# Four edits joined in a twelve-layer kernel: two exponentials on GpSimd, a summary in 64-column tiles, a second projection bank, and an earlier normalisation

## The reference, cut to what matters

```
L1_xattn: k = ctx @ Wk.T + bk; v = ctx @ Wv.T + bv           # ctx: 2 x 2048 tokens
          p = exp(clip(q.k / 4, -50, 50)) * keep; out = (p @ v) / (sum p + 1e-8)
L2_attn : attn = softmax(q k^T * scale); out = attn @ v; out @ wo      # 16 heads
L2_ffn  : h = down(silu(up(x))); q = W_q h; top-8 of 45 + 45 keys per head -> 8 experts for each of 8 heads
          z = h . down_embed[idx];  z = silu(z * softmax(sc));  x += z @ up_embed[idx]
L3_xattn: k' = relu(Wkf k) * mask; kv = k'^T v; k_sum = sum k'
          out = (q' kv) / (q' k_sum + 1e-8)                   # q' = relu(Wqf q), 2 x 2048 context tokens
```

## Time and profile before

| what | value |
|---|---|
| median of 3 runs | 1339.32 us (1335.14 to 1339.72) |
| profiled execution, its own time | 1336.76 us |
| its span, first to last instruction | 1334.9 us |
| busy share PE / DVE / ACT / POOL | 85% / 52% / 36% / 12% |
| mean granted TensorE clock | 0.919 of full speed |
| L1X, front to the last tile | 142 to 290 us |
| L2A, loop of units | 783 to 846 us |
| L2F with L3X | 847 to 1161 us |

### The profile page before, as it was taken

One profiled execution on the slowest core, in us unless ns is written; L12 is line 12 of the kernel. 1 busy time (PEld: TensorE's weight loads), 2 busy tenths in 40 slices (PEclk: granted clock), 3 DMA queues, 4 the chain that ended last, 5 costly groups with the idle time before them and its releaser, 6 DMA issues.

```text
span 1334.9 us, 22850 instructions
## 1 busy us (share of the span) xinstructions
PE 1140.2 (85%) x9353; PEld 817.2 (61%) x9353; DVE 696.4 (52%) x1532; ACT 482.1 (36%) x1069; POOL 165.4 (12%) x168
## 2 busy tenths in 40 slices
PE   6987889977877999999999977856986976777998
PEld 5866556656654555555556655735764755676886
DVE  3543456763326777655666253462626647374332
ACT  1101146762312355655566833222332321121322
POOL 0004000000001000000000000073635462000000
PEclk9998999998987999999999999977978957786999
DMA  9021200003003000000000020152524241003552
GB/s 365 1 95 48 111 1 1 2 2 154 0 16 135 1 2 2 1 2 1 2 2 2 2 77 1 54 145 63 152 70 123 78 113 48 14 0 158 198 204 81
DMA packets 16182, 84.38 MB, mean 63 GB/s; under 512 B 3152, under 2 KB 3664, under 8 KB 12368
## 3 DMA queue, kind: packets, MB, share of 16 engines
q1 hardware_dynamic: 7888, 57.75, 11.3%
q0 software_dynamic: 8192, 25.17, 6.7%
HBM read 82.65 MB, written 0.26 MB: 62 GB/s over the span
## 4 chain that ended last, share of the span: by engine, by line
PE 74%; DVE 12%; issue 5%; ACT 4%; another core or an unknown queue 3%; POOL 1%; DMA 1%; POOLq 0%; SPq 0%; DVEq 0%; ACTq 0%
PE L2X_bank_ring L1762 6%; PE L2X_bank_ring L1778 6%; PE L2X_bank_read L1792 5%; PE L2X_bank_ring L1701 4%; PE L2F_bank_sim L2389 3%; PE L1X_banks_scores L910 3%; PE L2X_bank_ring L1710 2%; PE L1X_bank_proj L887 2%; PE L0X_bank_k L457 2%; PE L2F_bank_keys L2347 2%; PE L3F_bank_y L3327 2%; PE L0X_bank_moments L468 2%; PE L2F_banks_pair L2364 2%; PE L3F_bank_gathered L3276 2%
## 5 line engine op out<-in xcount | busy, mean ns | idle before, releaser
L2059 DVE TENSOR_REDUCE L2X_max_parts<-L2X_bank_ring 128x1 f32<-128x512 f32 x256 | 158.3, 684 | 85.7 <-PE L2X_bank_ring L1762 85.7
L1970 ACT ACTIVATE L2X_context_exp<-L2X_bank_ring 128x384 f32<-128x384 f32 (+1 forms) x384 | 144.5, 465 | 62.1 <-PE L2X_bank_ring L1778 59.5
L2477 POOL DMA_INDIRECT L2F_rows<-in_L2F_embed_dram,L2F_expert x128 | 132.3, 1033 | 107.8 <-DVE x L2698 50.4
L1762 PE MATMUL L2X_bank_ring<-L2X_context_kT,L2X_q_masked 32*128 32x512 f32 x512 | 96.9, 630 | 0.0
L1016 ACT ACTIVATE L1X_probs<-L1X_clipped,L1X_drop,L1X_keep 128x1024 f32<-128x1024 f32 x64 | 77.9, 1240 | 32.1 <-DVE L1X_clipped L1075 24.9
L2389 PEld LDWEIGHTS L2F_bank_sim<-L3X_v_ones,L3X_k_features 128*128 128x128 f32 x512 | 72.1, 211 | 26.0 <-issue 24.2
L1075 DVE TENSOR_SCALAR L1X_clipped<-L1X_banks_scores 128x1024 f32<-128x1024 f32 x64 | 75.4, 1220 | 24.1 <-PE L1X_banks_scores L910 22.3
L2389 PE MATMUL L2F_bank_sim<-L3X_v_ones,L3X_k_features 128*128 128x34 f32 x512 | 69.2, 285 | 20.0 <-issue 19.8
L1778 PE MATMUL L2X_bank_ring<-L2X_q_and_max,L2X_context_kT 32*128 32x384 f32 (+1 forms) x768 | 86.0, 497 | 0.0
L1792 PEld LDWEIGHTS L2X_bank_read<-L2X_context_exp,L2X_context_v_ones 128*32 128x32 f32 x2048 | 50.2, 109 | 43.8 <-issue 33.4
L1792 PE MATMUL L2X_bank_read<-L2X_context_exp,L2X_context_v_ones 128*32 128x128 f32 x2048 | 75.8, 277 | 1.1 <-ACT L2X_context_exp L1970 0.8
(11 more groups left out here) (618 smaller groups left out, 2075.6 us busy)
## 6 DMA issues: line engine op xcount, KB each, us to landing
L3F_expert_weights<-in_L3F_experts_dram SPq DMA_DIRECT2D x16, 1280.0 KB, 5.6
L1A_groups<-in_L1A_groups_dram SPq DMA_DIRECT2D x3, 1536.0 KB, 9.6
ctxT<-in_ctxT_dram SPq DMA_DIRECT2D x8, 512.0 KB, 10.5
L0X_tokens<-in_L0X_tokens_dram SPq DMA_DIRECT2D x8, 512.0 KB, 15.0
slot<-in_L1A_dram SPq DMA_DIRECT2D x1, 3584.0 KB, 11.4
...
```

What stands on the lines that cost most here:

```text
L1762: nc.tensor.matmul(bank[:, :], qm[32 * g:32 * g + 32, b, c, j, :], cT[32 * g:32 * g + 32, s % 3, blk * 512:(blk + 1) * 512], start=True, s ...
L1970: nc.scalar.activation(ex[:, n % NE, g, 0:width(s)], bank_of(s_e, done(n) + g + 1)[:, 0:width(s)], ACT.Exp, scale=SCALE).then_inc(s_e, 1)
L2059: nc.vector.tensor_reduce(parts[:, j, g, blk:blk + 1], bank_of(s_ft, n)[:, :], AX, ALU.max).then_inc(s_ft, 1)
L2477: pool.indirect_dma_start(out=rows[:, r, k, :], out_offset=None, in_=env.dram["L2F_embed"], in_offset=bass.IndirectOffsetOnAxis(idx[:, b, ...
```

## The change: what it does

Four edits.

1. **L2F.** `exp_z` and `exp_soft` for parts 2 and 3 move from ACT to POOL, as `pow` of a tile of 1/e with z (or the shifted scores, now with the sign reversed) as the exponent. POOL takes `exp_z(n-2)` after the fourth gather of chunk n; the last three follow after all gathers. DVE's `products(m)` now stands ahead of `weighted_sum(m-1)`, with three z buffers in place of two. Ring buffers: three for the first nine chunks, then four. `norm3` is split in `moments3` and `norm3`.
2. **L3X.** The summary's operands change places: weights are 34 columns (two heads' values and ones), the moving operand is the 128 features, and even and odd head pairs write partitions 0 to 33 and 64 to 97. ACT copies the result (`copy_kv`), PE turns it back (`turn_kv`) before `kv_blocks`. Batch 0's stages 5 and 6 move behind the loop, among batch 1's; the wait for the last z goes, and the idle products are 10, ahead of them.
3. **L1X.** Batch 0's projections alternate between two banks each (`front_k`, `front_v`) and wait for the copy before the last. Batch 1's steps are spread to tile 27, TURN is 18; the ones in the value tile are set by two small memsets.
4. **L2A.** DVE's `normalise(n)` stands ahead of `maxima(n+1)`.

```diff
+    front_k, front_v = (bank_p, pair_s[2][:, 512:1024]), (bank_v, pair_s[1][:, 512:1024])
-    k_step = {2 * j: j for j in range(NJ)}
-    v_step = {2 * j + 5: j for j in range(NV)}
-    TURN = 2 * NV + 5
+    k_step = {n: j for j, n in enumerate((1, 3, 7, 10, 15, 19, 22, 26))}
+    v_step = {n: j for j, n in enumerate((5, 8, 12, 14, 17, 21, 24, 27))}
+    TURN = 18
         def project_k(b, j):
-            if b * NJ + j:
-                pe.wait_ge(s_kc, b * NJ + j)
+            if b == 0 and j >= 2:
+                pe.wait_ge(s_kc, j - 1)
...
-        chain(nc.vector.memset(vop[:, :, :], 1.0))
+        nc.vector.memset(vo[:, :, :, HD], 1.0)
+        chain(nc.vector.memset(vop[:, :, NH * VW:], 1.0))
...
-    ring = [0, 1, 2, 0, 1, 2, 3] + [n % 4 for n in range(len(chunks) - 7)]
+    ring = [n % 3 for n in range(9)] + [(n + 3) % 4 for n in range(len(chunks) - 9)]
...
             for j in range(NPAIR):
-                c, ct = divmod(j, 4)
-                i = nc.tensor.matmul(bank_kv[b][:, j * 2 * VW:(j + 1) * 2 * VW], kf[:, n % NB, j, :, :].rearrange("p r f -> p (r f)"),
-                                     vp[:, c, :, ct, :], start=(t == 0 and j == 0), stop=(t == NT - 1), skip_group_check=True)
+                lo, at = 64 * (j % 2), j // 2 * P
+                i = nc.tensor.matmul(bank_kv[b][lo:lo + 2 * VW, at:at + P], vo[:, n % NB, j * 2 * VW:(j + 1) * 2 * VW],
+                                     kf[:, n % NB, j, :, :].rearrange("p r f -> p (r f)"),
+                                     start=(t == 0 and j < 2), stop=(t == NT - 1), skip_group_check=True)
...
-        pe.wait_ge(s_vc, len(steps))
-        pe.wait_ge(s_z, len(pieces))
-        idle_products(M, bank_v, 24)
-        for n in range(7):
-            finish(1, n, bank_x, bank_p0, (bank_p1, bank_h), bank_p0)
-            if n in (0, 4, 5):
-                idle_products(M, bank_v, 4)
+        idle_products(M, bank_v, 10)
+        finish(1, 0, bank_k, bank_k, None, bank_k)
+        turn_kv(1)
+        finish(1, 1, bank_k, bank_k, None, bank_k)
+        finish(0, 5, bank_kv[0], None, None, None)
+        finish(1, 2, None, None, (bank_p0, bank_p1), None)
+        finish(1, 3, None, None, (bank_p0, bank_p1), None)
+        finish(0, 6, None, None, None, bank_kv[0])
+        finish(1, 4, None, None, None, None)
+        idle_products(M, bank_v, 4)
+        finish(1, 5, bank_k, None, None, None)
+        idle_products(M, bank_v, 4)
+        finish(1, 6, None, None, None, bank_k)
...
+        def exp_z(m):
+            _, lo, hi = pieces[m]
+            pool.wait_ge(s_z, m + 1)
+            nc.gpsimd.tensor_tensor(ze[:, m % 3, lo:hi], per_e[:, lo:hi], zz[:, m % 3, lo:hi], ALU.pow).then_inc(s_ze, 1)
...
+                if k == TOP // 2 - 1:
+                    if chunks[n] in [p[0:2] for p in parts[2:]]:
+                        exp_soft([p[0:2] for p in parts].index(chunks[n]))
+                    if n == 10:
+                        rstd3[0].gpsimd(pool)
+                    if n >= 2:
+                        exp_z(n - 2)
+        for m in range(len(chunks) - 2, len(pieces)):
+            exp_z(m)
...
-        def exp_z(m):
-            _, lo, hi = pieces[m]
-            act.wait_ge(s_z, m + 1)
-            nc.scalar.activation(ze[:, m % 2, lo:hi], zz[:, m % 2, lo:hi], ACT.Exp, scale=-1.0).then_inc(s_ze, 1)
+        def copy_kv(b):
+            act.wait_ge(s_sum, NT * (b + 1))
+            for lo in (0, 64):
+                i = nc.scalar.activation(kvT[lo:lo + 2 * VW, :], bank_kv[b][lo:lo + 2 * VW, :], ACT.Copy)
...
-        for m in range(len(pieces)):
-            if m == 4:
+        for m in range(len(pieces) + 1):
+            if m == 6:
                 natural_h(1, bank_e1)
                 choose(*parts[2], 5)
-            if m == 7:
+            if m == 9:
                 choose(*parts[3], 5)
...
-            products(m)
-            if m == 13:
-                divided(0)
-            weighted_sum(m)
-            if m == 14:
-                add_out(0, bank_k)
-                kv_blocks(1)
+            if m < len(pieces):
+                products(m)
+            if m:
+                weighted_sum(m - 1)
+            if m == 8:
+                moments3(0)
+            if m == 9:
+                norm3(0)
+        moments3(1)
         norm3(1)
+        divided(0)
+        kv_blocks(1)
+        add_out(0, bank_kv[0])
         divided(1)
-        add_out(1, bank_p0)
+        add_out(1, bank_k)
...
         for n in range(NU):
+            normalise(n)
             if n + 1 < NU:
                 maxima(n + 1)
             if n + AHEAD < NJ:
                 rotate(n + AHEAD)
-            normalise(n)
```

More of the change, by code:

```diff
@@ L864, in layer_L1X, with placed @@
     per = 2 * NT
-    k_step = {2 * j: j for j in range(NJ)}
-    v_step = {2 * j + 5: j for j in range(NV)}
-    TURN = 2 * NV + 5
+    k_step = {n: j for j, n in enumerate((1, 3, 7, 10, 15, 19, 22, 26))}
+    v_step = {n: j for j, n in enumerate((5, 8, 12, 14, 17, 21, 24, 27))}
+    TURN = 18
+    def placed(steps, n):
+        return sum(m < n for m in steps)
     env.prefetch(L, "L1A")
@@ L2460, in _, with exp_soft @@
         head.gpsimd(pool)
+        nc.gpsimd.memset(per_e[:, :], float(np.exp(-1.0))).then_inc(s_base, 1)
         L.clear_previous(pool)
+        def exp_z(m):
+            _, lo, hi = pieces[m]
+            pool.wait_ge(s_z, m + 1)
+            nc.gpsimd.tensor_tensor(ze[:, m % 3, lo:hi], per_e[:, lo:hi], zz[:, m % 3, lo:hi], ALU.pow).then_inc(s_ze, 1)
+        def exp_soft(part):
+            b, lo, hi = parts[part]
+            pool.wait_ge(s_sh, part + 1)
+            many = soft[:, b, lo:hi, :].rearrange("p h k -> p (h k)")
+            nc.gpsimd.tensor_tensor(many, per_e[:, 0:(hi - lo) * TOP], many, ALU.pow).then_inc(s_se, 1)
+        pool.wait_ge(s_base, 1)
         for n, (b, h) in enumerate(chunks):
@@ L2583, in _ @@
                 act.wait_ge(s_sh, 2)
-                exp_soft((0, 0, RH))
-            if n in (14, 20):
-                part = 2 if n == 14 else 3
-                act.wait_ge(s_sh, part + 1)
-                exp_soft(parts[part])
-            if n in exp_after:
-                exp_z(exp_after[n])
+                nc.scalar.activation(soft[:, 0, :, :], soft[:, 0, :, :], ACT.Exp, scale=-1.0).then_inc(s_se, 1)
             if n % 4 == 0 and n // 4 + 1 < len(steps) // 4:
@@ L2604, in _ @@
         head.vector(dve, chain)
+        nc.vector.memset(kvT[:, :], 0.0).then_inc(s_zero, 1)
         env.wait_weights(dve, "L2F")
@@ L2760, in _ @@
                 normalise(*parts[2], 2)
-                norm3(0)
             if m == 12:
```

108 lines of the change are left out of this document (63 added, 45 removed).

## The result

| | before | changed kernel |
|---|---|---|
| median of four runs each, first series | 1339.52 us | 1261.05 us |
| profiled execution: span | 1334.9 | 1258.2 |
| mean granted clock | 0.919 | 0.947 |

The account below looks back on a forecast made before the run. It took the bound to be L2F's gather chain, with DVE waiting for exponentials in ACT's list and POOL for ring buffers. Terms -44 + 0 - 7.6 - 8.4 = -60 gave span 1275, forecast 1277 us, range 1256 to 1302.

Parts of the forecast that it names:

- The time and its sign: Whole kernel: 1277 us, and faster by more than 6.7 us with chance 0.93, same 0.02, slower 0.05.
- The chunk model: L2F: POOL paces the gathers at 12.6 us a chunk, 17.9 with a softmax exponential; chunk 8 waits 4.3.
- the -44: L2F's gather chain: exponentials moved to POOL bring batch 1's normalised x from 1145.0 to 1096, 49 us less 5 for stalls.
- Rival 4: L2F: moving the exponentials does not free the chain, as a gather's landing or another wait paces it; 1305, chance 0.04.
- Rival 1: L2F with L3X: PE and its stalls set the end, the stage gains only 20 to 25 us; 1300, chance 0.09.
- Rival 2: L2F: POOL's powers and DVE's additions slow each other, +8 us; 1285, inside the forecast's 0.76 chance.
- Rival 3: L2F: the power costs by the element, 69 us more at the ceiling; 1346, chance 0.05.
- Rival 5: Better than the sum: no stalls, POOL at 10.0 us a chunk, full clock in the tail; 1258, chance 0.06.
- L1X's front: Start of L1X: two banks remove PE's waits for copies, 8.2 us, less 0.6 in the loop; -7.6, ends -9 and -5.
- L2A: Earlier normalisation on DVE cuts PE's 12.1 us of waits for probabilities; -8.4, ends -12 and -4.
- The tail: From batch 1's normalised x to x complete: idle products go, other work and a low clock come; 0, ends -5 and +5.
- The summary in 64-column tiles: L3X: eight matmuls fall from 1.87 to 1.1 to 1.3 us if tiles run side by side; gain counted as nothing.

Follow-up runs that it names:

- e7: The changed kernel with POOL's small power on one column of eight, the other seven filled once by a memset; 1241.8 us, ratio 0.969 to the kernel before.
- e8: The changed kernel with the two 32-column softmax exponentials given back from POOL to ACT; 1247.2 us, ratio 0.973 to the kernel before.
- e11: The changed kernel with PE held up twice by feature products repeated 18 times ahead of steps 4 and 20; 1277.8 us, ratio 0.950 to the kernel before.
- e6: The changed kernel run again without any edit; 1257.4 us, ratio 0.982 to the kernel before.
- e5: The kernel before, run again without any edit; 1280.3 us.

## Why the prediction was right, and where it was not

**The time and its sign** were right: 1277 (1256 to 1302) forecast, 1261 measured. For the changed kernel's own time that was no luck, since it stands at 1257 and 1261 at the two levels. For the gain it was in part: 62 us were forecast and 78 measured, but at the lower level the same change gives 23. The chunk model of the changed kernel held too: 12.6 us a chunk forecast and 12.3 measured, one wait of 6.1 ahead of chunk 8 (4.3 forecast), 210.1 us of gathers (213.6), 16.3 to the normalised x (15.6). e7 and e8 confirm POOL as the pace.

**The step that failed** is the reason for the -44: "DVE sat 78.9 us before it could use an exponential that ACT had in its list behind relu and copies of L3X". The place in the list was the path of the delay, not its source. The source was PE: idle 34.3 us in L2F with no releaser shown, and with signals that came up to 24 us behind its products. I had seen 19.8 of the idle time and booked it as an allowance on the other side, 5 us lost. The reading was also incomplete: POOL waited 50.4 us for the ring and 20.5 more for batch 0's variance, and the second wait is not in the prediction. At the level without stalls the same edits change the gather chain (first gather to normalised x) by +0.7 us: gathers +11.9, behind the last gather -11.2. At the level with stalls they bring 51.6. The changed kernel lies at 1257 and 1261 at the two levels, the kernel before at 1280 and 1340: what the edit buys is that most of the stalls stay off the chain.

**Rival 4** (the move does not free the chain: 1305, a gain of 32) was therefore the right picture of two series. The gain there was 23 us, since the gathers got longer, which I had not priced against a chain that runs well. **Rival 1** is refuted: PE's last summary ended at 1052.0, 18 us ahead of the normalised x (40 forecast). It comes true only in e11, with PE held up. **Rival 2** cost nothing that can be seen in the additions: 128 of them took 62.4 us in all, 62.2 before. By the rule of the Trainium skill (SBUF — State Buffer, "SBUF: two separate sides") a power and an addition would exclude each other. Where the power begins first, the trace of the changed kernel does not agree (view from 991 to 996 us): seven additions ran back to back, one every 0.52 us, three of them wholly inside a power that took its usual 1.68:

```profile
990.52 3.64 DVE L2745 SCALAR_TENSOR_TENSOR x<-L2F_rows,L2F_expert_weight,x 128x256 f32<-128x256 f32 x7
992.59 1.68 POOL L2492 TENSOR_TENSOR L2F_z_exp<-L2F_one_by_e,L2F_z 128x8 f32<-128x8 f32 x1
```

Where DVE begins first, e6 does agree, though with DVE's product of the gathered rows, and no power began behind the start of an addition:

```profile
988.98 1.22 DVE L2730 TENSOR_TENSOR L2F_rows<-L2F_rows,L2F_h 128x1024 f32<-128x1024 f32 x1
989.22 2.52 POOL L2492 TENSOR_TENSOR L2F_z_exp<-L2F_one_by_e,L2F_z 128x8 f32<-128x8 f32 x1
```

The power ends 1.53 us after the product, as if it had begun near the product's end. That costs little here: one power was 0.24 us longer in the changed kernel's first profile, and three were 1.5 us longer in all in e6. **Rival 3** is refuted by 1.68 us a power. **Rival 5** named nearly the right time by wrong terms: POOL needed 12.3 a chunk, not 10.0, and the tail's clock was 0.77.

**L1X's front**: -7.6 forecast. The step was right. From the first key projection to scores(0) it is 39.2 us in all five profiles without the edit and 30.8 in all nine with it, a gain of 8.45 (8.2 by the seven waits and the short one), and the 32 tiles take 0.5 more (0.6 forecast for the loop). The rest of the 10.9 us to L2A in the first pair is not of this edit: 1.1 stand ahead of L1X, where the nine profiles with the edit differ by 6.5 us, and 1.9 behind its tiles.

**L2A**: -8.4 forecast, -12.0 and -11.8 measured. The waits fell by 8.6, as the unit by unit count had it. The rest is the clock, 0.95 to 1.00, a term that the sum did not have.

**The tail**: 0 forecast, -2.6 and -3.1 measured. PE came in at a low clock as forecast (it had waited 16.1 us, and the tail's clock was 0.77, where it was 0.86 before), so I put the gain down to the missing idle products; no run has that edit alone. By their row they stood 3.5 us in the way, not 3.3.

**The summary in 64-column tiles** took 1.07 us where I had 1.1 to 1.3 and 1.87 was measured before. PE's busy time in this line fell from 69.2 to 37.7 us (65.1 in e5, without stalls). The Trainium skill (TensorEngine Tiling, "Key Properties") names a drain at each change of tiling mode; if there is one here, it is inside a gain of 0.8 us a step.
